# Ordering 50,000 edges in two levels of matrix products ahead of the edge stage of a graph network

## The reference, cut to what matters

```python
def edge_nn(x, W, b):
    h = relu(x @ W.T + b)
    return relu(h @ W.T + b)

h = maximum(layernorm(x), 0)                  # x: 50000 nodes x 256
S = h[src]                                    # 50000 edges
msgs = zeros_like(S)
for r in range(2):
    msgs = where((rel == r)[:, None], edge_nn(S, W_rel[r], b_rel[r]), msgs)
agg = segment_sum(msgs, dst, num_segments=50000)
gates = agg @ W_ih.T + b_ih + b_hh            # 1024 wide: i, f, g, o
i, f, g, o = split(gates, 4)
hn = sigmoid(o) * tanh(sigmoid(i) * tanh(g))
out = x + (relu(relu(hn @ W1.T + b1) @ W2.T + b2) @ W3.T + b3)
```

## Time and profile before

| | |
|---|---|
| median of 3 runs | 2703.93 us (2703.04 to 2705.19) |
| the profiled execution's own time | 2705.38 us |
| its span, first to last instruction | 2703.7 us |
| granted TensorE clock, mean | 0.921 |
| busy: PE / DVE / ACT / POOL | 84% / 69% / 61% / 41% |
| memory moved | 392.62 MB, mean 145 GB/s |

### The profile page before, as it was taken

One profiled execution on the slowest core, in us unless ns is written; L12 is line 12 of the kernel. 1 busy time (PEld: TensorE's weight loads), 2 busy tenths in 40 slices (PEclk: granted clock), 3 DMA queues, 4 the chain that ended last, 5 costly groups with the idle time before them and its releaser, 6 DMA issues.

```text
span 2703.7 us, 50650 instructions
## 1 busy us (share of the span) xinstructions
PE 2276.7 (84%) x14435; PEld 1494.0 (55%) x14436; DVE 1861.0 (69%) x4659; ACT 1661.1 (61%) x3695; POOL 1119.3 (41%) x909
## 2 busy tenths in 40 slices
PE   5457787788877788777777859999999999999997
PEld 2345566566666666666656735555555555555553
DVE  7445665666765667655655638888888888888886
ACT  5446666566666667655656646666666666666663
POOL 0357677766777766777777620000000000000000
PEclk9788988899988989888888879999999999999998
DMA  9965455544555545555555547888888888888886
GB/s 362 373 197 90 85 92 96 94 82 80 91 97 95 89 80 87 98 95 91 89 96 96 86 88 168 187 190 190 190 191 192 192 189 189 189 191 190 191 194 148
DMA packets 382327, 392.62 MB, mean 145 GB/s; under 512 B 259333, under 2 KB 312853, under 8 KB 376087
## 3 DMA queue, kind: packets, MB, share of 16 engines
q0 software_dynamic: 90912, 156.30, 34.8%
q1 hardware_dynamic: 288803, 234.97, 31.3%
q10 hardware_dynamic: 2516, 0.14, 0.1%
HBM read 183.79 MB, written 155.92 MB: 126 GB/s over the span
## 4 chain that ended last, share of the span: by engine, by line
PE 64%; ACT 15%; issue 7%; another core or an unknown queue 6%; DMA 5%; SPq 1%; DVE 1%; POOL 1%; ACTq 0%; POOLq 0%; DVEq 0%
PE bank L1170 28%; PE bank L1105 7%; PE bank L1138 6%; PE bank L1182 5%; PE bank L1200 5%; PE bank L1121 4%; DMA agg<-zeros 4%; ACT xn L676 3%; PE bank L1089 3%; ACT count_tmp L659 3%; ACT hot_tile L626 3%; ACT summed L647 2%; PE bank L1190 2%; PE bank L1042 2%
## 5 line engine op out<-in xcount | busy, mean ns | idle before, releaser
L577 POOL DMA_INDIRECT agg<-summed,scatter_idx x400 | 637.5, 1594 | 348.7 <-ACT summed L647 173.4
L1170 PE MATMUL bank<-a_hi,ihT 128*128 128x512 f16 x2352 | 701.8, 380 | 28.8 <-DMA a_lo<-row_lo 28.8
L600 POOL DMA_DIRECT2D y<-in_x x98 | 84.0, 857 | 1023.2 <-DVE y L975 1001.5
L589 POOL DMA_INDIRECT xg<-in_x,src_ring x400 | 396.5, 991 | 202.6 <-issue 117.2
L1170 PE MATMUL bank<-a_lo,ihT 128*128 128x512 f16 x1176 | 446.7, 380 | 0.0
L1170 PEld LDWEIGHTS bank<-a_hi,ihT 128*128 128x128 f16 x2352 | 230.6, 98 | 307.7 <-issue 31.6
L1089 PE MATMUL bank<-ident,xn 128*128 128x128 f32 x800 | 149.2, 317 | 237.5 <-ACT xn L676 132.1
L1105 PE MATMUL bank<-s_hi,relT 128*128 128x256 f16 x1600 | 342.8, 312 | 0.0
L879 DVE SCALAR_TENSOR_TENSOR s_lo<-bank,s_hi 128x512 f16<-128x512 f32 x200 | 136.3, 682 | 296.0 <-ACT s_hi L652 256.8
L1121 PE MATMUL bank<-relT,h_hi 128*128 x1600 | 332.3, 281 | 0.1
L1089 PEld LDWEIGHTS bank<-ident,xn 128*128 128x128 f32 x800 | 104.3, 161 | 293.1 <-ACT xn L676 146.5
(11 more groups left out here) (138 smaller groups left out, 4888.3 us busy)
## 6 DMA issues: line engine op xcount, KB each, us to landing
agg<-zeros SPq DMA_DIRECT2D x24, 2112.0 KB
agg_in<-agg SPq DMA_DIRECT2D x98, 512.0 KB, 4.7
y<-in_x POOLq DMA_DIRECT2D x98, 512.0 KB, 8.2
out<-y SPq DMA_DIRECT2D x98, 512.0 KB, 7.9
dst_ring<-dst_rows SPq DMA_DIRECT2D x100, 256.0 KB
xg<-in_x,src_ring POOLq DMA_INDIRECT x400
agg<-summed,scatter_idx POOLq DMA_INDIRECT x400
src_ring<-src_slot SPq DMA_DIRECT2D x200, 1.0 KB
```

Of the source, the lines that this page charges most:

```text
L577: nc.gpsimd.indirect_dma_start(out=agg[:, :], out_offset=bass.IndirectOffsetOnAxis(ap=scatter_idx[:, e.slot(8), t % 2:t % 2 + 1], axis=0), ...
L589: nc.gpsimd.indirect_dma_start(out=xg[:, k.slot(8), t, :], out_offset=None, in_=x[:, :], in_offset=bass.IndirectOffsetOnAxis(ap=src_ring[: ...
L1170: last = nc.tensor.matmul(N_C[c % 3][:, :], lhs, rhs, start=i == 0, stop=i == len(todo) - 1)
```

## The change

The ordering is replaced as a whole and stands wholly ahead of the edge stage; `at.batch()`, the block work in the steps and the extra pieces of loop go (one loop, steps 16 to 184). An edge's class is its relation and the quarter of the nodes that holds its destination, eight classes. The edges lie as 400 columns of 125 edges. Within a column the edges of one class take neighbouring slots, so at most two tiles, and a column has 16 such windows (`WINDOWS`). Level one: one product for each column, one-hot lanes (125x128) with the three parts sorted by window (125x48). Level two: the 48 results of 100 columns are turned round by products with an identity and then multiplied with one-hots of tiles 100 wide, added into one bank for each part at a column offset held in a register.

```diff
+COLS = EDGES // ROWS
+GROUP = 100
+COL_GROUPS = COLS // GROUP
+CLASSES = NUM_REL * QUARTERS
+PAIRS = -(-(EDGES + QUARTERS * (PAIR - 1)) // (2 * PAIR)) * 2
-BATCH = 4
+WINDOWS = 2 * CLASSES
+WV = PARTS * WINDOWS
+BATCH = 10
+BATCHES = GROUP // BATCH
+TURNS = WV // 4
+SPAN = (GROUP * ROWS + 2 * P - 2) // P + 1
-ZERO_EARLY = 11
+ZERO_FLIGHT = 3
-        B_T, B_P, B_H, B_M, B_G = (bank[0], bank[1], bank[2:4], bank[4:6], bank[6:8])
+        B_T, B_H, B_M, B_G = (bank[0:2], bank[2:4], bank[4:6], bank[6:8])
+        E_COLS, E_TURN, E_PLACE = bank[0:3], bank[3:5], bank[5:8]
-        EDGE_RUN = dict(loops=((16, 32), (40, 56), (56, 80), (88, 104), (104, 128), (136, PAIRS - 16)), unroll=8)
+        EDGE_RUN = dict(loops=((16, PAIRS - 16),), unroll=8)
```

So there are 400 columns in 4 groups, 8 classes, 16 windows, 48 window parts, 40 batches of 10 columns, 12 turns in a group, and spans of 100 tiles; `PAIRS` is 200 as before. SyncE reads the edges in runs of 2000 bytes and goes on to the zeroing at once, up to three pieces in flight; the weights load from ACT's queue:

```diff
+            for i, t in enumerate((rel, dst, src)):
+                sp.dma_start(edge_i[:, i, :, :], t.rearrange("(p q e) -> p q e", q=COL_GROUPS, e=ROWS)).then_inc(edges_in, 16)
             sp.wait_ge(zero_tile, 1)
-            sp.wait_ge(edges_in, 48)
-            sp.wait_ge(weights_in, 16 * WEIGHT_LOADS)
+            for i in range(ZERO_DMAS):
+                if i >= ZERO_FLIGHT:
+                    sp.wait_ge(agg_zeroed[i % ZERO_FLIGHT], 16 * (i // ZERO_FLIGHT))
```

VectorE finds the classes (3 casts of 125x500 or 100x500, 4 instructions of 125x400 for the quarter and class, 8 for the one-hots of the classes), the starts of the classes (22 instructions on a few numbers, each waiting for the one before), and the slots (8 instructions of 125x400 on the ranks that TensorE makes with 40 products of 400 columns); then for each group of columns:

```diff
+            def windows(i):
+                cols = slice(i * GROUP, (i + 1) * GROUP)
+                chained(nc.vector.tensor_tensor(hot_win[:, :, :], iota_win[:, :, :],
+                                                win16[:, cols].unsqueeze(1).to_broadcast([ROWS, WINDOWS, GROUP]),
+                                                ALU.is_equal))
+                wait_from(dve, cols_done, (i - 1) * BATCHES)
+                nc.vector.tensor_tensor(win_parts[:, i % 2, :, :, :],
+                                                hot_win[:, :, :].unsqueeze(1).to_broadcast([ROWS, PARTS, WINDOWS, GROUP]),
+                                                parts16[:, :, cols].unsqueeze(2).to_broadcast([ROWS, PARTS, WINDOWS, GROUP]),
+                                                ALU.mult).then_inc(win_ready, 1)
+            def lanes(n):
+                wait_from(dve, cols_done, n - HOT_SLOTS + 1)
+                nc.vector.tensor_tensor(hot_lane[:, n % HOT_SLOTS, :, :], iota_lane[:, :, :],
+                                        lane16[:, n * BATCH:(n + 1) * BATCH].unsqueeze(1).to_broadcast([ROWS, P, BATCH]),
+                                        ALU.is_equal).then_inc(lane_ready, 1)
+            def tiles(i):
+                wait_from(dve, piece_done, (i - 1) * BATCHES)
+                for w in range(WINDOWS):
+                    last = nc.vector.tensor_scalar(hot_tile[:, i % 2, w, :], iota_span[:, :],
+                                                   win_tile[:, i, w // 2, w % 2:w % 2 + 1], None, ALU.is_equal)
+                last.then_inc(tile_ready, 1)
```

`windows` has 1600 and 4800 elements a partition, `lanes` 1280. ScalarE copies between the levels, TensorE multiplies:

```diff
+            def cols_copy(n):
+                act.wait_ge(cols_done, n + 1)
+                i, b = n // BATCHES, n % BATCHES
+                wait_from(act, turn_done, (i - 1) * TURNS)
+                nc.scalar.copy(col_parts[:, i % 2, :, b * BATCH:(b + 1) * BATCH],
+                               E_COLS[n % 3][:, 0:BATCH * WV].rearrange("p (c w) -> p w c", c=BATCH)).then_inc(cols_out, 1)
+            def turn_copy(i, g):
+                act.wait_ge(turn_done, i * TURNS + g + 1)
+                wait_from(act, piece_done, (i - 1) * BATCHES)
+                nc.scalar.copy(turned_parts[:, i % 2, g * 4:(g + 1) * 4, :].rearrange("p w l -> p (w l)"),
+                               E_TURN[g % 2][0:GROUP, :]).then_inc(turn_out, 1)
```

```diff
+            def columns(n):
+                i, b = n // BATCHES, n % BATCHES
+                pe.wait_ge(win_ready, i + 1)
+                pe.wait_ge(lane_ready, n + 1)
+                wait_from(pe, cols_out, n - 2)
+                for c in range(BATCH):
+                    last = nc.tensor.matmul(E_COLS[n % 3][:, c * WV:(c + 1) * WV], hot_lane[:, n % HOT_SLOTS, :, c],
+                                            win_parts[:, i % 2, :, :, b * BATCH + c].rearrange("p n w -> p (n w)"),
+                                            start=True, stop=True)
+                last.then_inc(cols_done, 1)
+            def turn(i, g):
+                pe.wait_ge(cols_out, (i + 1) * BATCHES)
+                wait_from(pe, turn_out, i * TURNS + g - 1)
+                for w in range(4):
+                    last = nc.tensor.matmul(E_TURN[g % 2][0:GROUP, w * P:(w + 1) * P], col_parts[:, i % 2, g * 4 + w, :],
+                                            ident16[:, :], start=True, stop=True)
+                last.then_inc(turn_done, 1)
+            def clear(start):
+                for n in range(PARTS):
+                    last = nc.tensor.matmul(E_PLACE[n][:, :], no16[:, 0:P], no16[:, :], start=start, stop=not start)
+                return last
+            def piece(i, b, at_tile):
+                if b == 0:
+                    pe.wait_ge(turn_out, (i + 1) * TURNS)
+                    pe.wait_ge(tile_ready, i + 1)
+                for w in range(b * WINDOWS // BATCHES, (b + 1) * WINDOWS // BATCHES):
+                    for n in range(PARTS):
+                        last = nc.tensor.matmul(E_PLACE[n][:, bass.ds(at_tile[w // 2], SPAN)],
+                                                turned_parts[:, i % 2, n * WINDOWS + w, :], hot_tile[:, i % 2, w, :],
+                                                start=False, stop=False)
+                last.then_inc(piece_done, 1)
+            pe.wait_ge(rank_read, CLASSES)
+            clear(True)
+            for i in range(COL_GROUPS + 1):
+                if i:
+                    _, at_tile = nc.values_load_multi_w_load_instructions(
+                        first_tile[0:1, i - 1, :], engines=[mybir.EngineType.PE], min_val=0, max_val=TILES - 1)
+                for b in range(BATCHES):
+                    if i < COL_GROUPS:
+                        columns(i * BATCHES + b)
+                    if i:
+                        piece(i - 1, b, at_tile)
+                if i < COL_GROUPS:
+                    if i == 0:
+                        pe.wait_ge(sums_read, 1)
+                        pe.wait_ge(first_ready, 1)
+                    for g in range(TURNS):
+                        turn(i, g)
+            clear(False).then_inc(piece_done, 1)
```

Then come the decoding in one block of 400 tiles (`src_slots_ready`), the turning of the destinations, and only now the transposes of the weights, which stood before the ordering. In the edge step of TensorE:

```diff
-                    wait_from(pe, s_ready, k.n)
-                            last = nc.tensor.transpose(B_T[:, c:c + P],
+                            last = nc.tensor.transpose(B_T[k.slot(2)][:, c:c + P],
```

More of the change, by code:

```diff
@@ L123, in is_ @@
         return isinstance(self.j, int) and self.n == n
[L125 to L131, removed]
     @property
@@ L651, in step @@
                     act.wait_ge(s_turned, k.n + 1)
[L652 removed]
+                    nc.scalar.activation(s_hi[:, k.slot(2), :], B_T[k.slot(2)][:, :], ACT.Relu).then_inc(s_hi_ready, 1)
                 k = at - 3
@@ new lines, in _ @@
+            for k in range(CLASSES):
+                dve.wait_ge(rank_done, k + 1)
+                y_k = E_RANK[k % 4][0:ROWS, 0:COLS]
+                if k == 0:
+                    last = nc.vector.tensor_scalar(slot[:, :], y_k, base_of(k), None, ALU.add)
+                else:
+                    dve.wait_ge(rank_read, k)
+                    last = nc.vector.scalar_tensor_tensor(out=slot[:, :], in0=y_k, scalar=base_of(k), in1=slot[:, :],
+                                                          op0=ALU.add, op1=ALU.max)
+                last.then_inc(rank_read, 1)
@@ new lines, in _ @@
+            for j in range(COL_GROUPS):
+                for i in range(j + 1):
+                    last = nc.tensor.matmul(E_SUM[0:GROUP, 128 + j * CLASSES:128 + (j + 1) * CLASSES],
+                                            behind[:, i, j * GROUP:(j + 1) * GROUP], totals[:, i, :], start=i == 0, stop=i == j)
+            for j in range(COL_GROUPS):
+                c = 256 + j * CLASSES
+                if j == 0:
+                    last = nc.tensor.matmul(E_SUM[:, c:c + CLASSES], no16[:, 0:P], no16[:, 0:CLASSES], start=True, stop=True)
+                for i in range(j):
+                    last = nc.tensor.matmul(E_SUM[:, c:c + CLASSES], ones16[0:GROUP, 0:P], totals[:, i, :],
+                                            start=i == 0, stop=i == j - 1)
@@ new lines, in _ @@
+            last.then_inc(sums_done, 1)
+            for k in range(CLASSES):
+                wait_from(pe, rank_read, k - 3)
+                y_k = E_RANK[k % 4][0:ROWS, 0:COLS]
+                nc.tensor.matmul(y_k, fold[:, :], in_class[:, k, :], start=True, stop=False)
+                for i in range(COL_GROUPS):
+                    last = nc.tensor.matmul(y_k, totals[:, i, k:k + 1].to_broadcast([GROUP, ROWS]), behind[:, i, :], start=False, stop=i == COL_GROUPS - 1)
+                last.then_inc(rank_done, 1)
```

581 lines of the change are left out of this document (311 added, 270 removed).

## The result

The changed kernel is slower: 2722.91 us median (2718.69 to 2728.82, 4 runs) against 2703.48 (2701.97 to 2705.19), ratio 1.0073, 95% interval 1.0051 to 1.0096. The forecast was 2695 and faster. The profiled execution took 2720.12 us, its span is 2718.4.

A forecast was written before the change was run, and what follows sets the result against it. TensorE bounds the node stage; in the edge stage no engine is full and POOL waits for PE, ACT and DVE. (146 + 42 - 160.6) - 39.4 + 3 = -9 from 2705.4 gives 2696, median 2695 us; range 2662 to 2730.

The forecast's parts named there:

- T: Moment when `src_slot` of block 0 is ready in the changed kernel: 146 us forecast, bounds 120 and 194.
- step 1: New ordering until T: first windows at 37 us, then four groups of placement at 0.107 us a load, 146 in all.
- step 3: From T to the first scatter: 42 us, so 188 instead of 160.63, +27.4; bounds 36 and 50.
- step 4: Edge stage: 84 quads fall from 14.67 to 14.20 us each, -39.4; the first quads cost +3.
- rival B: Slower placement, TensorE at 1.2 GHz or loads and products in sequence: T 167 to 194, 2716 to 2743 us, chance 0.2.
- Rival E: Faster placement, a load under a short product takes half, registers hidden: T 118 to 134, 2667 to 2683 us, chance 0.13.
- step 2: Zeroing from 3 us, three pieces in flight, ends at 125 to 130; the 47.50 us wait goes, no cost elsewhere.
- Rivals C: Edge stage without placement: the chain gets ahead of POOL, which runs at 12.6 us a quad; 2561 us, chance 0.07.
- D: Edge stage: the pace stays 14.67 us a quad, 14.20 being owed to place in the old order; 2734 us, chance 0.1.
- step 5: Two banks for `s` in the edge stage: worth 0, bounds -1.0 us a quad and 0.
- step 6: The buffers' new addresses and the edges' new order: 0, bounds plus or minus 0.3 us a quad.
- break-even T = 155: The value of T at which the changed kernel was to take as long as the kernel before.

The follow-up runs named there:

- e1: The changed kernel, but SyncE waits until all weights have landed before it issues the first piece of zeroing: 2693.07 us, ratio 0.9972.
- e2: The changed kernel with the 14 weight loads moved behind ScalarE's loop of copies: 2692.48 us, ratio 0.9955.
- e6: The kernel of e2, but VectorE copies the results of every second turn: ratio 0.9975.
- e9: The kernel of e5 with four banks for the turns instead of two: ratio 0.9938.
- e4: The kernel of e2 with idle products of 512 columns, two ahead of each batch of columns, one ahead of each turn: ratio 1.0043.
- e5: The kernel of e2, but the first eight pairs are gathered four pairs ahead instead of eight: ratio 0.9943.
- e3: The changed kernel with one bank for the transposes and TensorE's wait for `s_ready` of the pair before: 2724.72 us, ratio 1.009.
- e12: The changed kernel with two pieces of zeroing in flight instead of three: ratio 1.0046.
- e8: The changed kernel with one piece of zeroing in flight instead of three: ratio 1.0092.
- e14: The kernel of e11 with the weight loads issued on GpSimd's queue, the zeroing starting at 3 us: 2659.01 us, ratio 0.9904.
- e11: The kernel of e9 with VectorE copying every second turn and the registers read ahead of the turns: ratio 0.9938.
- e13: The kernel of e11 with the weight loads as in e1, issued by ScalarE first while the zeroing waits for them: ratio 0.9952.

## Why the prediction was wrong

**The step that failed is the sum of T (step 1), by a term that it did not have.** It priced DVE, TensorE and ScalarE's 22 copies a group, and never counted the fourteen weight loads that the diff moves into ScalarE's program ahead of its first copy, nor what their issue costs beside three pieces of zeroing in flight. ScalarE started 31.5 us late; T was 167.9 instead of 146. e1 and e2 take just that away and give 139.9 to 141.6 and 2692 to 2693 us, where the forecast had 2695. So the missing term is 28 us (167.9 against e2's 139.9), and the rest of the sum of T was 6 too high. From the sum (2696) to the profiled 2720.1 it is 24 us: 21.9 in T, 9.0 in step 3 and -7.0 in step 4. The last two nearly cancel, so that e1 and e2 meet the 2695 is in part luck.

- *To the slots*: first columns due at 37, multiplied at 35.05, 2 us early.
- *The placement*: a group 25.3 expected, 24.8 measured (88.09 to 112.92). Two errors cancel. A turn cost 0.70, not 0.55, since the bank's round trip bounds it (e6, e9); a batch with its piece 1.31, not 1.58: ten columns 0.93, not 1.07, and a piece 0.38, not 0.51. Registers and what surrounds them: 3.2 to 4.1, 2.9 expected.
- *The clock*: 0.9 or more expected, 0.50 measured. The condition of rival B came true, its price didn't: a pair of short products took 0.08 to 0.107 there, not 0.22. The sum read one price for load and product, 0.11, out of the earlier trace rows, whose 128-column products are float32 transposes; with float16 the same width takes half, 0.107 at 1.2 GHz and 0.053 at 2.4 (e4). So "the load sets the pitch" was a wrong reading, and for the turns 0.107 came out right only because the clock was half of what the sum assumed. Rival E's load at half the price came true for turns and pieces, at a clock that the placement never had. At the lower clock alone T is 140 (e2). 2722.9 us lies in B's band by accident.
- *Zeroing* (step 2): last piece issued at 119.6, first scatter no longer waits. Right for `agg`; that the zeroing "costs nothing elsewhere" was the fault's other half. "Only edges and weights use memory then" named the weights, but asked only how long they take, not whose program stands still while they are issued.
- *From T to the first scatter* (step 3): 42 expected, 51.0 measured. The sum took the fill's pace, 5.4 a step, from the row at 105.57 on, and had no term for the stall of about 10 us just before it. From the second `s_hi` to the first `h_hi` it was 13.2 us in the kernel before (89.57 to 102.79), 13.1 in the changed kernel and 13.9 in e2, against 3.0 in e5.
- *The pace* (step 4): 36.4 us net expected, 43.4 measured. The first six quads cost 5.0 more (3 expected), the 84 in the middle 42.6 less (39.4), and the last nine, which had no term, 5.8 less. The pitch from quad 20 to 90 is 14.16, as forecast (14.2). Rivals C and D are out: that mean is neither near 12.6 nor at 14.67.
- *The bank* (step 5): nothing, as expected (e3). The new addresses and the new order of the edges (step 6) had no run of their own; the middle pitch of 14.16 leaves them little room.

The break-even T = 155 held, with the errors of steps 3 and 4 in it that nearly cancel (with both as measured it is 153): T = 141.6 is faster, 162 (e12) and 167.9 are slower. It counts only where nothing else holds the first gather: e8 has T = 138.5 and is slower.

## What to carry to other kernels

When DMAs change their queue, write down each engine's program with its DMA issues in it, and ask for each issue what fills the queues at that moment; one issue beside three pieces of zeroing cost ScalarE 20.9 us where it costs 0.6 alone. Give such loads to an engine that nobody waits for; on GpSimd the fourteen took 9.8 us in all beside the same zeroing (e14). After each gain ask again what stands in that queue: the same loads took back 10 us of the next improvement (e11 against e13), and then the zeroing itself became the bound.

## What the runs showed of the hardware

A weight load with its short float16 product took 0.107 us (128 columns streamed), 0.080 (100) and 0.093 (48) at 1.2 GHz, and 0.053, 0.048 and 0.092 at 2.4 (e4, e9). The Trainium skill ("TensorE: Matmul & The Clock Gate", section "LDWEIGHTS (loading the stationary operand)") gives a load's columns divided by 1.2 as its nanoseconds, by which a load of 128 columns would take 107 (an estimate by that rule); the trace disagrees: the loads of `hot_lane` and `turned_parts` have 128 columns, and with their products they follow one another by 0.093 and 0.080 us at 1.2 GHz, and by 0.048 for `turned_parts` at 2.4.

One piece of zeroing of 2.1 MB in flight left ScalarE's issues at 0.4 to 5.2 us and all fourteen over by 19 us; with two and three they were over at 61 and 68 us (e8, e12, the changed kernel). The last piece of zeroing was issued by 126 and 120 us with two and three in flight, by 169 with one.
